# Expert tiles: one of the four result transfers of a tile moved ahead of the second low part on POOL, with waits for ACT's high parts between the transfers

## The chip, the cores and the metric

The kernel runs on one core of one Trainium2 chip. The metric is the device time of one execution in microseconds. The kernel uses all engines of the core: TensorE (PE in the rows, PEld for its weight loads), VectorE (DVE), ScalarE (ACT), GpSimd (POOL) and SyncE (SP), each with its own program and in order; they meet only through semaphores.

## The reference

A network of layers on an input of 32 images of 16 x 16 pixels with 64 channels: a windowed attention, an involution convolution, a linear attention over tokens, a mixture of experts routed per image, another linear attention, and last a mixture of experts routed per token. The change lies in the last one:

```python
flat = x.reshape(-1, C)                      # 8192 tokens, C = 64
probs = softmax(flat @ router_w.T)           # 8 experts
topk_probs, topk_idx = top_k(probs, 2)       # then normalised
h1 = einsum('nc,ehc->neh', flat, w1)         # H = 682
h3 = einsum('nc,ehc->neh', flat, w3)
h = silu(h1) * h3
y = einsum('neh,ech->nec', h, w2)
out = einsum('ne,nec->nc', gates, y)
```

## The kernel before

Each token is sent to the slots of its two experts in a scratch tensor, so that every expert's tokens stand together. The work is then cut into NT = 39 tiles of 512 slots. For a tile t the hidden dimension is cut into NHB = 6 blocks of 114 (index k = 0 to 5), and one block goes through all engines:

- **up product** (TensorE, L2123, four matmuls of 512 columns) into two PSUM banks;
- **silu** (ACT, L1630) of the first bank, then the product with the second (DVE, L1331), the hidden value in float32;
- **high part** (ACT, L1613): the hidden value rounded to float16; the semaphore `high5` counts them, so that `high5` at t * 6 + k + 1 means that the high part of block k of tile t is made;
- **low part**: what the rounding left, hidden value less high part, in float16. For k = 0, 1, 3, 4 DVE makes it (L1341), for k = 2 and 5 POOL (L722, `low5_pool`);
- **down product** (TensorE, L2104, eight matmuls of 128 columns), which waits for the low part. It is issued three blocks behind the up product, so those of k = 3, 4, 5 stand in the next tile, behind its up products of k = 0, 1, 2.

After the last down product of a tile ACT copies one half of the result (L1621) and DVE adds the other (L1347, semaphore `y5`), both in the next tile. At k = 4 TensorE transposes the next tile's input (L2093) and ACT copies it (L1607), from which the next tile's first up product reads.

POOL then sends the 512 finished rows out by four indirect transfers of 128 rows (L710, `results5`), to places that a small copy of ids (L704, `ids5`) made earlier. POOL's program is written out tile by tile in order of t, with no loop. TensorE, ACT and DVE run tiles 2 to 37 in a loop whose turn takes two tiles, an even and an odd one; the tiles at both ends are written out. SP loads the input of a tile (L543) once the input of two tiles before was transposed and its ids copied. After the last transfer has landed, SP loads all results back, and DVE and POOL mix them and write the output.

Of the kernel before, what the change touches and what calls it, by code (L numbers as in the profile page):

```python
# [27 lines left out]
HB, NHB = 114, 6  # L28
# [7 lines left out]
NT = (4 * COLS + E * (SLOTS - 1)) // SLOTS  # L36
# [75 lines left out]
def network(nc, xw_d, xi_d, mats_d, vecs_d, feats_d, cw1_d, wmask_d, taps_d, wexp_d,  # L112
            w1l2_d, w2l2_d, w1l3_d, w3l3_d, w2l3_d, out_d, slots_d, results_d):
    with ExitStack() as ctx:
# [5 lines left out]
        def S(step):  # L120

            name = PLACE.get(step, (step, 0))[0]
            if name not in sems:
                sems[name] = nc.alloc_semaphore(name)
            return sems[name]

        def when(step, n):

            return S(step), PLACE.get(step, (step, 0))[1] + n
# [439 lines left out]
        def _(pool):  # L569
# [130 lines left out]
            def ids5(t):  # L700
                if t >= 4:
                    pool.wait_ge(*when(f"resulted_{t % 2}", 16 * SUB * (t // 2 - 1)))
                pool.wait_ge(*when(f"loaded_xs_{t % 2}", 16 * (t // 2 + 1)))
                nc.gpsimd.tensor_copy(IDS[t % 4], XS[t % 2].bitcast(U32)[:, :, C]).then_inc(S("ids5"), 1)  # L704

            def results5(t, subs):
                pool.wait_ge(*when("y5", t + 1))
                pool.wait_ge(*when("ids5", t + 1))
                for i in subs:
                    pool.indirect_dma_start(  # L710
                        results_d, bass.IndirectOffsetOnAxis(ap=IDS[t % 4][:, i:i + 1], axis=0),
                        Y5[t % 2][:, i, :], None).then_inc(S(f"resulted_{t % 2}"), 16)
# [4 lines left out]
            def low5_pool(t, k):  # L717
                n = t * NHB + k
                pool.wait_ge(*when("high5", n + 1))
                if n >= 3:  # L720
                    pool.wait_ge(*when("down5", n - 2))
                nc.gpsimd.tensor_tensor(LO5[k % 3], H5[k % 3], HI5[k % 3], ALU.subtract).then_inc(S("low5_pool"), 1)  # L722

            for t in range(NT + 1):
                if t < NT:
                    low5_pool(t, 2)
                if t >= 1:
                    results5(t - 1, (0, 1))
                if t < NT:
                    low5_pool(t, 5)  # L730
                if t >= 1:
                    results5(t - 1, (2, 3))
                    if t + 1 < NT:
                        ids5(t + 1)
            for c in (1, 3, 5):
# [1575 lines left out]
```

## Time and profile before

| | us |
|---|---|
| median of three timed runs | 1309.49 (1305.29 to 1313.16) |
| the profiled execution, its own time | 1303.19 |
| its span, first to last instruction | 1301.2 |
| busy in the span: PE, DVE, ACT, POOL | 998.1, 854.9, 689.0, 648.7 |
| stretch of the 39 tiles | about 906 to 1268 |

The rows below are of this one profiled execution, and times in them count from the start of its span. Busy time of an engine doesn't say that it sets the pace; the idle time in brackets behind a row, with what ended it, and the distance between starts say more. "issue" stands for idle time that the profile can't put down to another engine. Times on POOL are rough, so its work is best read by the distance of starts.

### The profile page before, as it was taken

The numbers are of one execution on the slowest core, as the hardware profiler recorded it, in microseconds if no ns is written. First come the engines' busy times: TensorE is split into PE (matmuls) and PEld (weight loads), VectorE is DVE, ScalarE is ACT, GpSimd is POOL, SyncE is SP. The second block draws the span as 40 slices with busy tenths as digits, with TensorE's granted clock in tenths as the row PEclk, the third lists the DMA queues.
The fourth block names the chain that finished last, engine by engine and source line by source line (L and its number), as shares of the span: only waits on it lengthen the run. The fifth ranks groups of instructions, "written<-read, shape, count | busy, mean of one in ns | idle before, by whom it ended". The sixth has DMA issues, their size and how long they took to land.

```text
span 1301.2 us, 23386 instructions
## 1 busy us (share of the span) xinstructions
PE 998.1 (77%) x6350; PEld 631.7 (49%) x6351; DVE 854.9 (66%) x1864; ACT 689.0 (53%) x1311; POOL 648.7 (50%) x722
## 2 busy tenths in 40 slices
PE   5779999948996986667787656521999999999970
PEld 3347777723446752233354334210666666666640
DVE  7977777778857325645746555550777777777757
ACT  2714444405462366555665443211888888878860
POOL 3924545422778202000404456574576767767775
PEclk9979999978998798777898887755999999999995
DMA  5000000010004000000200000011001011010105
GB/s 190 2 1 0 0 0 0 0 60 1 1 28 126 21 1 0 1 0 0 68 5 16 17 20 22 19 36 49 23 26 32 26 31 32 26 32 27 31 22 194
DMA packets 24261, 38.55 MB, mean 30 GB/s; under 512 B 6212, under 2 KB 14168, under 8 KB 23960
## 3 DMA queue, kind: packets, MB, share of 16 engines
q1 hardware_dynamic: 15128, 28.62, 7.0%
q0 software_dynamic: 9088, 9.39, 2.3%
q8 instruction: 21, 0.34, 0.1%
q14 instruction: 24, 0.20, 0.1%
HBM read 24.52 MB, written 13.47 MB: 29 GB/s over the span
## 4 chain that ended last, share of the span: by engine, by line
PE 38%; POOL 17%; DVE 17%; issue 16%; ACT 7%; another core or an unknown queue 2%; SPq 1%; DMA 1%; DVEq 0%; POOLq 0%; ACTq 0%
POOL results L710 10%; POOL stage L722 6%; PE bank L1707 5%; PE bank L1724 4%; PE bank L1716 2%; PE bank L1709 2%; PE bank L1766 2%; PE bank L1931 2%; PE bank L1896 2%; PE bank L1732 1%; DVE T L800 1%; PE bank L1779 1%; PE bank L1915 1%; PE bank L1814 1%
## 5 line engine op out<-in xcount | busy, mean ns | idle before, releaser
L2123 PE MATMUL bank<-stage,big 128*114 128x512 f16 x936 | 244.4, 384 | 21.5 <-issue 20.6
L1331 DVE TENSOR_TENSOR T<-bank,T 114x512 f32<-114x512 f32 x234 | 161.6, 691 | 120.7 <-ACT T L1630 120.2
L687 POOL DMA_INDIRECT slots<-T,index x128 | 124.5, 972 | 118.4 <-DVE index L1242 81.9
L1630 ACT ACTIVATE T<-bank 114x512 f32<-114x512 f32 x234 | 139.8, 597 | 66.1 <-PE bank L2123 43.8
L710 POOL DMA_INDIRECT results<-stage,small x156 | 152.8, 980 | 37.7 <-issue 37.7
L2104 PEld LDWEIGHTS bank<-l2w,stage 114*128 114x128 f16 x1872 | 121.1, 98 | 58.2 <-issue 19.2
L1613 ACT ACTIVATE stage<-T 114x512 f16<-114x512 f32 x234 | 146.1, 625 | 0.3 <-DVE T L1331 0.3
L2104 PE MATMUL bank<-l2w,stage 114*128 x1872 | 143.6, 219 | 1.8 <-POOL stage L722 0.8
L2123 PEld LDWEIGHTS bank<-stage,big 128*114 x936 | 108.6, 132 | 67.9 <-issue 30.8
L722 POOL TENSOR_TENSOR stage<-T,stage 114x512 f16<-114x512 f32 x78 | 90.0, 1153 | 74.4 <-ACT stage L1613 65.2
L1341 DVE TENSOR_TENSOR stage<-T,stage 114x512 f16<-114x512 f32 x156 | 106.3, 681 | 0.0
L1397 ACT ACTIVATE stage<-stage 128x512 f32<-128x512 f32 x64 | 40.3, 630 | 118.8 <-DVE stage L825 118.8
L613 POOL TENSOR_TENSOR stage<-T,vecs 128x128 f32<-128x128 f32 x64 | 26.4, 412 | 105.3 <-PE bank L1709 105.3
L1707 PE MATMUL bank<-stage 128*128 128x512 f32 x128 | 70.0, 628 | 6.7 <-DVE big L810 6.7
L634 POOL TENSOR_TENSOR stage<-stage 128x512 f16<-128x512 f32 x40 | 46.0, 1158 | 51.8 <-ACT stage L1431 50.8
L822 DVE TENSOR_REDUCE small<-bank 128x8 f32<-128x512 f32 x64 | 44.3, 692 | 36.0 <-PE bank L1709 36.0
L617 POOL TENSOR_TENSOR stage<-T,small 128x512 f32<-128x512 f32 x64 | 67.6, 1056 | 0.0
L1724 PE MATMUL bank<-big,stage 128*128 (+1 forms) x512 | 62.8, 268 | 0.0
L1724 PEld LDWEIGHTS bank<-big,stage 128*128 128x128 f32 x512 | 62.2, 192 | 0.1
L1931 PE MATMUL bank<-T,mats 128*128 128x512 f32 x64 | 42.6, 763 | 20.2 <-ACT T L1520 13.6
L672 POOL MEMSET stage<- 128x2080 f32 x1 | 1.8, 1831 | 106.7 <-DVE T L1095 106.7
L1507 ACT ACTIVATE stage<-bank,small 128x256 f32<-128x256 f32 x64 | 30.3, 473 | 43.1 <-PE bank L1915 40.8
(384 smaller groups left out, 2134.4 us busy)
## 6 DMA issues: line engine op xcount, KB each, us to landing
stage<-slots SPq DMA_DIRECT2D x39, 130.0 KB
stage<-in_w1l SPq DMA_DIRECT2D x8, 342.0 KB
stage<-in_w3l SPq DMA_DIRECT2D x8, 342.0 KB
results<-stage,small POOLq DMA_INDIRECT x156
T<-in_xw SPq DMA_DIRECT2D x4, 512.0 KB, 6.9
X<-in_xi SPq DMA_DIRECT2D x1, 2048.0 KB, 14.9
slots<-T,index POOLq DMA_INDIRECT x128
A<-results SPq DMA_DIRECT2D x4, 512.0 KB, 6.6
```

The source lines that it names most:

```text
L687: pool.indirect_dma_start(slots_d, bass.IndirectOffsetOnAxis(ap=index[:, k, n:n + 1], axis=0), rows5[:, n * RW:(n + 1) * RW], None).then_i ...
L710: pool.indirect_dma_start(results_d, bass.IndirectOffsetOnAxis(ap=IDS[t % 4][:, i:i + 1], axis=0), Y5[t % 2][:, i, :], None).then_inc(S(f" ...
L722: nc.gpsimd.tensor_tensor(LO5[k % 3], H5[k % 3], HI5[k % 3], ALU.subtract).then_inc(S("low5_pool"), 1)
L1331: nc.vector.tensor_tensor(H5[q], bank[3 + q][0:HB, :], S5[q], ALU.mult).then_inc(S("hid5"), 1)
L1341: nc.vector.tensor_tensor(LO5[q], H5[q], HI5[q], ALU.subtract).then_inc(S("low5"), 1)
L1613: nc.scalar.activation(HI5[q], H5[q], ACT.Copy).then_inc(S("high5"), 1)
L1630: nc.scalar.activation(S5[q], bank[q][0:HB, :], ACT.Silu).then_inc(S("silu5"), 1)
L1707: nc.tensor.matmul(bank[s][:, :], QB[s], KX[s], start=True, stop=False)
L1724: mm = nc.tensor.matmul(bank[4 + s][:, g * VW:(g + 1) * VW], PT[s][:, g * 128:(g + 1) * 128], VX[:, bass.ds(n * HP + g, 1), :].rearrange(" ...
L1931: nc.tensor.matmul(out, mat("mean"), T2P[c], start=True, stop=True).then_inc(S4(op), 1)
L2104: mm = nc.tensor.matmul(bank[6 + s][:, i * 128:(i + 1) * 128], H[:, i * 128:(i + 1) * 128], downs[:, bass.ds(w, 2 * C)], start=(k == 0 and ...
L2123: mm = nc.tensor.matmul(bank[q + 3 * (v // 2)][0:HB, :], big16[:, bass.ds(e * (4 * HID3) + (v * HID3 + k * HB), HB)], XT[s], start=(v % 2 ...
```

## The change

Before, POOL's program for tile t is: low part of block 2, transfers 0 and 1 of tile t - 1, low part of block 5, transfers 2 and 3, copy of the ids of tile t + 1. After it, transfers 0, 1 and 2 stand between the two low parts, and transfer 3 behind the second. Ahead of transfer 1 POOL waits for `high5` at t * 6 + 4 (block 3 of tile t, counted from 0), ahead of transfer 2 for t * 6 + 5 (block 4). In the last round (t = NT, no tile left) there are no such waits. As `results5` is now called for one transfer at a time, its own two waits (`y5`, `ids5`) are repeated for each.

```diff
                 if t < NT:
                     low5_pool(t, 2)
                 if t >= 1:
-                    results5(t - 1, (0, 1))
+                    for i in range(3):
+                        if i and t < NT:
+                            pool.wait_ge(*when("high5", t * NHB + 3 + i))
+                        results5(t - 1, (i,))
                 if t < NT:
                     low5_pool(t, 5)
                 if t >= 1:
-                    results5(t - 1, (2, 3))
+                    results5(t - 1, (3,))
                     if t + 1 < NT:
                         ids5(t + 1)
```

## Rows read from the trace of the kernel before

**Rows 1.** The page: shares of the chain that ended last, by line.

```profile
POOL results L710 10%; POOL stage L722 6%; PE bank L1707 5%; PE bank L1724 4%; PE bank L1716 2%; PE bank L1709 2%; PE bank L1766 2%; PE bank L1931 2%; PE bank L1896 2%; PE bank L1732 1%; DVE T L800 1%; PE bank L1779 1%; PE bank L1915 1%; PE bank L1814 1%
```

**Rows 2.** Tiles' stretch: busy (PE, PEld, DVE, ACT, POOL), PEclk, DMA; a wait's total, times.

```profile
912.68:1255.99 343.31, 322.73 (x2903) 224.22 (x2902) 257.24 (x421) 280.26 (x535) 240.04 (x261) 1.00 0.10 28
...
POOL stage L722 <- ACT stage L1613: 65.2, 40, 8.1
```

**Rows 3.** POOL's timeline, tile 14: start, duration, line, work, [idle before].

```profile
1039.82 1.15 POOL L722 TENSOR_TENSOR stage<-T,stage 114x512 f16<-114x512 f32 x1 [0.25 <-issue]
1041.13 1.00 POOL L710 DMA_INDIRECT results<-stage,small  x1 [0.16 <-issue]
1042.44 0.96 POOL L710 DMA_INDIRECT results<-stage,small  x1 [0.30 <-issue]
1044.48 1.15 POOL L722 TENSOR_TENSOR stage<-T,stage 114x512 f16<-114x512 f32 x1 [1.08 <-ACT stage L1613]
1045.79 0.99 POOL L710 DMA_INDIRECT results<-stage,small  x1 [0.16 <-issue]
1047.09 0.97 POOL L710 DMA_INDIRECT results<-stage,small  x1 [0.31 <-issue]
...
1048.49 1.16 POOL L722 TENSOR_TENSOR stage<-T,stage 114x512 f16<-114x512 f32 x1 [0.24 <-issue]
```

**Rows 4.** The other engines' timeline in the same stretch.

```profile
1042.03 0.64 ACT L1613 ACTIVATE stage<-T 114x512 f16<-114x512 f32 x1
...
1043.78 0.62 ACT L1613 ACTIVATE stage<-T 114x512 f16<-114x512 f32 x1
...
1044.77 1.03 PE L2123 MATMUL bank<-stage,big 128*114 128x512 f16 x4
...
1045.78 0.62 PE L2104 MATMUL bank<-l2w,stage 114*128 x8
...
1045.92 0.68 DVE L1341 TENSOR_TENSOR stage<-T,stage 114x512 f16<-114x512 f32 x1
...
1046.23 1.03 PE L2123 MATMUL bank<-stage,big 128*114 128x512 f16 x4
...
1047.10 0.61 PE L2104 MATMUL bank<-l2w,stage 114*128 x8
...
1047.79 0.62 ACT L1613 ACTIVATE stage<-T 114x512 f16<-114x512 f32 x1
```

**Rows 5.** POOL's timeline, tile 29, an odd one.

```profile
1174.85 1.15 POOL L722 TENSOR_TENSOR stage<-T,stage 114x512 f16<-114x512 f32 x1 [0.25 <-issue]
...
1178.70 0.96 POOL L710 DMA_INDIRECT results<-stage,small  x1 [1.54 <-issue]
1180.21 1.16 POOL L722 TENSOR_TENSOR stage<-T,stage 114x512 f16<-114x512 f32 x1 [0.54 <-ACT stage L1613]
```

**Rows 6.** Timeline of all engines, the last tile.

```profile
1255.99 1.15 POOL L722 TENSOR_TENSOR stage<-T,stage 114x512 f16<-114x512 f32 x1 [0.24 <-issue]
...
1258.61 0.96 POOL L710 DMA_INDIRECT results<-stage,small  x1 [0.30 <-issue]
...
1259.60 1.17 POOL L722 TENSOR_TENSOR stage<-T,stage 114x512 f16<-114x512 f32 x1
...
1261.97 0.42 DVE L1347 TENSOR_TENSOR stage<-stage,bank 128x256 f32<-128x256 f32 x1 [2.61 <-ACT stage L1621]
...
1263.50 0.97 POOL L710 DMA_INDIRECT results<-stage,small  x1 [0.30 <-issue]
1264.77 0.97 POOL L710 DMA_INDIRECT results<-stage,small  x1 [0.30 <-issue]
1266.04 0.97 POOL L710 DMA_INDIRECT results<-stage,small  x1 [0.30 <-issue]
```

**Rows 7.** The last stage: DVE beside POOL, and alone.

```profile
1287.71 1.53 DVE L1357 TENSOR_TENSOR X<-X,small 128x512 f32<-128x512 f32 x1
...
1296.59 0.68 DVE L1357 TENSOR_TENSOR X<-X,small 128x512 f32<-128x512 f32 x1
```

## The prediction

> **What bounds the kernel now.** I read the page first: no engine is busy all the way, and POOL's transfer line (L710) and low-part line (L722) head the chain that ended last, with 10% and 6% [rows 1]. That invites the thought that POOL sets the pace where the change is. The stretch with the expert tiles must decide, so I took its busy times: in 343.3 us TensorE is busy 322.7 at a granted clock of 1.00 (2.4 GHz), ACT 280, DVE 257, POOL 240 [rows 2]. TensorE is the engine near its limit, POOL has a third of the time free.
>
> Next, POOL's own timeline through one tile [rows 3]. The low part of block 2 starts at 1039.82, two transfers follow, and the queue then stands idle 1.08 us until ACT's high part of block 5 exists (1043.78 + 0.62 = 1044.40; POOL starts 0.08 later, at 1044.48) [rows 3, 4]. The other low part (1048.49) has a gap of 0.24 filed under issue, but it too starts 0.08 after an ACT high part: 1047.79 + 0.62 = 1048.41 [rows 3, 4]. So both low parts are now started by ACT, neither by POOL's queue. The chain's shares name POOL because it was followed back along POOL's own order; they are no room to gain.
>
> Last, what waits for POOL. TensorE's up product of block 2 starts at 1044.77; in tile after tile the down product comes 0.87 after an up product (1046.23 to 1047.10). Here it comes 1.01 after, at 1045.78, which is 0.15 behind the end of POOL's low part (1044.48 + 1.15 = 1045.63) [rows 3, 4]. So the down product of block 5 already waits for POOL, by 0.14 us, and that low part has no slack: whatever it is late by, TensorE is late by. Of the 39 down products behind POOL's other low part none is put down as waiting for it before the last tile.
>
> The distance between the two low parts of a tile is set by ACT and TensorE and has two sizes: about 4.66 us in even tiles (1039.82 to 1044.48 is tile 14; there are eighteen, t = 2 to 36, between 4.63 and 4.70) and 5.36 in odd ones (1174.85 to 1180.21), where the loop of TensorE turns over [rows 3, 5]. From the second low part to the next tile's first it is 4.01 (1044.48 to 1048.49) [rows 3]. The outliers at the ends are t = 0 (no transfers), t = 1 and t = 37 (5.09 and 4.94 in the same view).
>
> **The change, part by part.** It adds two waits per tile and moves one transfer of four from behind the second low part to in front of it. No transfer is added.
>
> *The two waits.* They stand for the high parts with index 3 and 4 of tile t. Index 3 is ready before index 4, and index 4 is ready 2.85 us after the first low part starts (1042.03 + 0.64 = 1042.67) [rows 3, 4]. The second transfer starts 2.62 after it (1042.44), over a microsecond behind index 3, and the third can't start before 3.90 [rows 3]. So neither wait holds: hidden by POOL's own work. If instead they held, by ACT being 1.05 later, they would push the transfer and the low part behind it. The waits as instructions: in the tail, the transfer behind the two repeated waits (1266.04) starts 1.27 after the one before, the one with no wait between (1264.77) 1.27 as well [rows 6]. A satisfied wait is free to within 0.01. For three ahead of one transfer I take 0; the upper end is in a rival.
>
> *The moved transfer.* I add start-to-start distances: low part to first transfer 1.31, to the second 1.31, to the third 1.28 (between 1.30, as 1045.79 to 1047.09, and the tail's 1.27) [rows 3, 6], transfer to low part 0.99. The last is seen once where POOL itself was late: 1258.61 to 1259.60, no idle time put down [rows 6]. The sum is 4.89 us. In even tiles 4.66 are there, so the low part of block 5 comes 0.23 late. In odd tiles 4.89 is under 5.36: nothing. In t = 1 and 37 it just fits. Bounds for the late part: gap from transfer to low part between 0.03 (this row) and 0.30 (a transfer behind a transfer) [rows 3]; that is 0.23 to 0.50 per even tile.
>
> *Does it pass on?* The down product of block 5 moves by the same 0.23, and the up product of block 3 behind it. ACT turns to the silu of block 3 as that product ends (1046.23 + 1.03 = 1047.26) and makes the high part of block 2, which starts the next low part, at 1047.79 [rows 4]; a cover of 0.1 at most can hide there (my estimate: the silu takes 0.6, so it began about when the product ended). I count 0.23 in full: 18 x 0.23 = 4.1 us. Lower bound: ACT's cover hides 0.1 each time, 18 x 0.1 = 1.8 less.
>
> The Trainium skill ("SBUF — State Buffer", section "Who interferes with whom") says that a DVE instruction with two SBUF inputs and a GpSimd instruction that reads SBUF exclude one another. The trace of the last stage agrees: L1357 takes 1.53 us beside POOL and 0.68 alone [rows 7]. By that rule the later low part (ending 1045.86) would come within 0.06 of DVE's L1341 at 1045.92 and could hold it 0.1 or 0.2; the down product that needs it is at 1047.10, 0.50 after its end at 1046.60, so the sum is 4.4 us by the rule and without it.
>
> *What moves earlier.* Behind the second low part only one transfer and the copy of the ids remain: 1.31 + 0.99 + 0.20 of 4.01 us. The copy comes about a microsecond earlier; the load of a later tile that it frees is not waited for. The first low part stays ACT's, so this buys nothing.
>
> *The tail.* In the last tile POOL already was the limit (3.61 us between low parts, 1255.99 to 1259.60) [rows 6]. With three transfers it is 4.89, so 1260.88, 1.28 late. Behind it stand the down product, ACT's copy and DVE's sum, with nothing else to do: the sum, before at 1261.97 for 0.42 us, ends at 1263.67, and the first transfer of the last tile starts at some 1263.8 instead of 1263.50 [rows 6]. The other delays are made up, since POOL had a queue of transfers to work off: +0.3 us.
>
> *A hiccup.* Once in the stretch a transfer came 1.24 late (idle 1.54 against 0.30) and the wait for ACT swallowed it [rows 5]. After the change the same thing between the low parts costs 4.89 + 1.24 - 5.36 = 0.8, or 1.24 in an even tile. I leave it out of the sum and keep it in the range.
>
> Sum: 4.1 + 0.3 = 4.4 us. The profiled execution took 1303.19 us (span 1301.2), so its like would take 1307.6; the median of the three timed runs is 1309.49, 6.3 above it. I predict against the median: 1313.9 us, 0.34% more. A measurement of this kernel tells about 0.5%, 6.5 us, from no change.
>
> **The rivals.**
> - *Later by more.* The gap before the low part is the 0.24 that stands between copy and low part [rows 3], or the three waits cost 0.1 together each time. Then the sum is 5.10, late by 0.44: 18 x 0.44 = 7.9, t = 1 and 37 give 0.2, the tail 0.5: 1318.1 us, slower by 0.66%. For it: that gap is there in every tile. Against it: it ends 0.08 after ACT's high part, and the only gap in which POOL was late is 0.03. It passes 0.5% from 0.34 us per even tile.
> - *Hidden.* The two sizes, 4.66 and 5.36, show that TensorE's loop turn costs 0.7 us every second tile [rows 3, 5]. If that time runs from something earlier than TensorE's last product, the lateness of the tile before vanishes in it. Then 0 to 2 us, 1310.5. Against it: the turn stands in TensorE's own program, behind that product and behind all that was late.
> - *Faster.* If the first low part is in truth held by POOL's queue and the 0.24 before it is its cost, the lighter second half starts it earlier and relieves the down product behind it; and if the 0.14 stall at block 5 went in 37 tiles as well, 5.2 us would be won: 1304.3. It decides only if POOL can start the low part of block 5 before 1044.48, and ACT's high part excludes that: 65.2 us of waiting for L1613 stand against it, in 40 waits [rows 2].
> - *No such order.* That ACT's high parts come late enough to hold the transfers needs index 4 about 1 us later than [rows 4] show before the waits bind at all; bound by 1 us more, the second low part would be late by 1.2 us in an even tile and 0.5 in an odd one, 31 us in all: 1340.
>
> **How the numbers follow.** My forecast (slower by 2.5 to 6 us) 0.58, later by more 0.17, hidden 0.13, faster 0.10, waits that bind 0.02. The range leaves that last one out and takes in the larger gap with a hiccup (1318.1 + 1.2 = 1319.3, and up to 1321 for the scatter of medians) and the hidden case with as much scatter below: 1307 to 1321. The faster rival's 5.2 us are just short of 0.5%, so with scatter and a larger relief I give 0.07 of its 0.10 to faster by over 0.5%; slower by over 0.5% is the 0.19 of the two slow rivals and 0.06 of my own case's upper scatter, 0.25; the rest, 0.68, is within 0.5%.
>
> **What the changed profile would show.** Right: in even tiles three L710 behind the first L722, 1.3 apart, and the second L722 4.9 us after the first with next to no idle time before it and no ACT named; in odd tiles 5.35 as before, with idle time of some 0.4; no transfer waiting for L1613; the down product 0.15 behind the end of that L722; two tiles in 18.27 instead of 18.04 us; behind the second L722 an idle time of over 1 us. Wrong: even distances of 5.1 (first rival), a pair of tiles still 18.04 (hidden) or shorter (faster), or transfers with an ACT wait before them.

## The result, and the profile after

The changed kernel takes 1319.63 us (median of 7 runs, 1315.16 to 1326.39), the kernel before 1310.83 (7 runs on the same chip): ratio of the means 1.0077, 95% interval 1.0047 to 1.0106, so 10 us slower and between 6 and 14 (the medians lie 8.8 apart). The forecast was 1313.9, slower by 4.4 us, and 1319.63 is in its range; but 0.77% is over the 0.5% within which the prediction put its largest chance (0.68), and falls in the 0.25 for slower. The direction and the delay that was worked out are there. The size is about twice the forecast's, and the profile shows a second delay that the prediction doesn't have.

The profiled execution of the changed kernel is the longest of its seven: 1326.39 us, span 1324.4. Its first low part starts at 923.20, against 914.1 in the trace of before: 9.1 of the 23.2 us between the two profiled executions lie ahead of the tiles, where nothing was changed. What counts is the tiles' stretch, from the first low part to the last. It was 345.5 us and is 360.4, and what follows the last low part is 0.8 shorter (40.8 against 41.6), so the traces put 14.1 us on the change, at the upper end of the interval.

First the stretch's busy times, as in [rows 2] but from the first low part to the last, the same of the kernel before (second view), and the waits in it in the changed kernel (in the changed kernel each line behind the edit has a number 3 higher: L1613 is L1616, L2104 is L2107, L2123 is L2126).

```profile
923.20:1283.60 360.40, 328.43 (x2926) 222.57 (x2924) 258.03 (x423) 276.92 (x537) 253.35 (x266) 1.00 0.09 27
```

```profile
914.08:1259.60 345.52, 323.96 (x2919) 224.96 (x2918) 258.60 (x423) 281.87 (x537) 243.16 (x265) 1.00 0.10 28
```

```profile
POOL stage L722 <- ACT stage L1616: 77.4, 60, 7.3
...
ACT T L1633 <- PE bank L2126: 71.8, 110, 1.5
...
PE bank L2107 <- POOL stage L722: 7.4, 19, 0.9
...
PE bank L2107 <- DVE stage L1344: 6.2, 19, 0.7
```

The work is the same and the clock is still 1.00 (2.4 GHz). POOL is busy 10 us longer, most of it in the copy of the ids (0.68 us in place of 0.20 in the even tiles); it has that time free. The stretch is 15 us longer because TensorE waits. Two waits come nineteen times each: for POOL's low part (forecast), in the eighteen even tiles and in tile 29, and for DVE's (not forecast), in sixteen of the even tiles and at the two ends. POOL's timeline of tile 14 answers to [rows 3]:

```profile
1053.35 1.16 POOL L722 TENSOR_TENSOR stage<-T,stage 114x512 f16<-114x512 f32 x1 [1.48 <-ACT stage L1616]
1054.66 1.00 POOL L710 DMA_INDIRECT results<-stage,small  x1 [0.15 <-issue]
1055.97 0.97 POOL L710 DMA_INDIRECT results<-stage,small  x1 [0.30 <-issue]
1057.24 0.97 POOL L710 DMA_INDIRECT results<-stage,small  x1 [0.30 <-issue]
1058.23 1.17 POOL L722 TENSOR_TENSOR stage<-T,stage 114x512 f16<-114x512 f32 x1
1059.56 0.99 POOL L710 DMA_INDIRECT results<-stage,small  x1 [0.16 <-issue]
1060.55 0.65 POOL L704 COPY small<-stage 128x4 uint32<-128x4 uint32 x1
```

The second low part is 4.88 us behind the first (forecast 4.89), right behind the third transfer, with no idle time and no engine named: POOL's own queue starts it now, where ACT did. No transfer waits for ACT. The other engines in the same tile show the second delay:

```profile
1056.90 1.03 PE L2126 MATMUL bank<-stage,big 128*114 128x512 f16 x4
...
1058.21 1.03 PE L2126 MATMUL bank<-stage,big 128*114 128x512 f16 x4
1059.16 0.60 ACT L1633 ACTIVATE T<-bank 114x512 f32<-114x512 f32 x1 [1.22 <-PE bank L2126]
...
1060.48 0.68 DVE L1344 TENSOR_TENSOR stage<-T,stage 114x512 f16<-114x512 f32 x1
...
1061.31 0.62 PE L2107 MATMUL bank<-l2w,stage 114*128 x8 [0.29 <-DVE stage L1344]
```

The up product that starts at 1056.90 ends at 1057.93, but ACT's silu of it starts at 1059.16, 1.2 us later, and ACT was idle for all of that. The silu's product and low part on DVE are late with it, and the down product at 1061.31 waits. That lengthens the distance from the second low part to the next tile's first from 4.01 to 4.44 in the median (4.41 here, 1058.23 to 1062.64). In odd tiles everything is as forecast: below, the third transfer, and then the low part still started by ACT, 0.56 after POOL came free (5.39 from the first, against 5.36):

```profile
1066.54 0.97 POOL L710 DMA_INDIRECT results<-stage,small  x1 [0.30 <-issue]
1068.07 1.15 POOL L722 TENSOR_TENSOR stage<-T,stage 114x512 f16<-114x512 f32 x1 [0.56 <-ACT stage L1616]
```

The last tile, which answers to [rows 6]:

```profile
1283.59 1.17 POOL L722 TENSOR_TENSOR stage<-T,stage 114x512 f16<-114x512 f32 x1
1284.90 0.66 PE L2107 MATMUL bank<-l2w,stage 114*128 x8 [2.09 <-POOL stage L722]
...
1286.01 0.42 DVE L1350 TENSOR_TENSOR stage<-stage,bank 128x256 f32<-128x256 f32 x1 [3.96 <-ACT stage L1624]
1286.70 0.97 POOL L710 DMA_INDIRECT results<-stage,small  x1 [0.79 <-DVE stage L1350]
```

The low part is 4.89 behind the one before (3.61 in [rows 6]), and the first transfer of the last tile starts 3.11 after it (1283.59 to 1286.70) where it was 3.90 (1259.60 to 1263.50): late by 1.28, and 0.8 made up again.

### The profile page after: what moved, and what is told of

It is laid out like the page before. It is cut to its first block, busy times and chain, and to the rows that moved or that the text cites. A ratio compares the mean times of both kernels' runs of the same rounds, so it can differ in the third digit from the quotient of the medians.

```text
span 1324.4 us, 23464 instructions
## 1 busy us (share of the span) xinstructions
PE 1002.2 (76%) x6350; PEld 630.1 (48%) x6351; DVE 855.9 (65%) x1864; ACT 683.4 (52%) x1311; POOL 657.3 (50%) x722
## 4 chain that ended last, share of the span: by engine, by line
issue 38%; PE 30%; DVE 12%; POOL 11%; ACT 5%; DMA 2%; SPq 1%; DVEq 0%; POOLq 0%; ACTq 0%
POOL results L710 6%; PE bank L1710 4%; PE bank L1727 4%; POOL stage L722 3%; PE bank L1719 2%; PE bank L1712 2%; PE bank L1769 2%; PE bank L1899 2%; POOL small L704 1%; PE bank L1735 1%; DVE T L803 1%; PE bank L1782 1%; PE bank L1817 1%; PE bank L1918 1%; DVE small L263 1%
## 5 line engine op out<-in xcount | busy, mean ns | idle before, releaser
L2126 PE MATMUL bank<-stage,big 128*114 128x512 f16 x936 | 243.4, 383 | 18.5 <-issue 15.8
L2107 PEld LDWEIGHTS bank<-l2w,stage 114*128 114x128 f16 x1872 | 118.1, 98 | 79.3 <-issue 53.4
L2107 PE MATMUL bank<-l2w,stage 114*128 x1872 | 143.7, 219 | 15.9 <-POOL stage L722 9.5
L1616 ACT ACTIVATE stage<-T 114x512 f16<-114x512 f32 x234 | 146.6, 626 | 0.2 <-DVE T L1334 0.2
L2126 PEld LDWEIGHTS bank<-stage,big 128*114 x936 | 108.1, 131 | 64.4 <-issue 27.0
L1344 DVE TENSOR_TENSOR stage<-T,stage 114x512 f16<-114x512 f32 x156 | 106.8, 685 | 0.0
L898 DVE TENSOR_TENSOR stage<-bank,big 128x512 f32<-128x512 f32 x72 | 46.9, 688 | 8.8 <-PE bank L1782 6.5
```

Source lines behind the costliest of these rows:

```text
L1344: nc.vector.tensor_tensor(LO5[q], H5[q], HI5[q], ALU.subtract).then_inc(S("low5"), 1)
L1616: nc.scalar.activation(HI5[q], H5[q], ACT.Copy).then_inc(S("high5"), 1)
L2107: mm = nc.tensor.matmul(bank[6 + s][:, i * 128:(i + 1) * 128], H[:, i * 128:(i + 1) * 128], downs[:, bass.ds(w, 2 * C)], start=(k == 0 and ...
L2126: mm = nc.tensor.matmul(bank[q + 3 * (v // 2)][0:HB, :], big16[:, bass.ds(e * (4 * HID3) + (v * HID3 + k * HB), HB)], XT[s], start=(v % 2 ...
```

## The experiments

The ratios compare each with the kernel before on the same chip in the same session. There the kernel before took 1262.17 us (e1 to e4), 1263.92 (e5, e6), 1262.59 (e7b to e9b) and 1303.94 (e10 to e12). Of the kernel before there are two traces only, "before" and e5, so the distances of e1 to e4 and e7b to e9b are read against those of e5. The names in the expectations are: LATE, the late low part of block 5 alone; SIGNALS, TensorE's results being told late while POOL works on transfers directly in a row; WAITS, the added waits.

The table has the distances between POOL's low parts (median; "in" from a tile's first to its second, "out" from there to the next tile's first), the length of a pair of tiles, and the stretch from the first low part to the last.

```
kernel            even in + out  odd in + out   pair   stretch  ratio of times [95%]
before            4.66 + 4.01    5.35 + 4.02    18.05  345.5    
after             4.88 + 4.44    5.39 + 4.01    18.71  360.4    1.0077 [1.0047, 1.0106]
e5 before again   4.53 + 4.01    5.36 + 4.01    17.91  343.2
e6 after again    4.88 + 4.03    5.36 + 4.01    18.28  352.1    1.0049 [1.0031, 1.0068]
e1 order only     4.88 + 4.03    5.36 + 4.01    18.29  352.1    1.0079 [1.0056, 1.0101]
e2 waits only     4.59 + 4.01    5.41 + 4.01    18.02  345.3    1.0021 [1.0001, 1.0041]
e3 filler         4.78 + 4.17    5.53 + 4.02    18.75  360.2    1.0115 [1.0073, 1.0157]
e4 paced pair     4.53 + 4.02    5.36 + 4.02    17.93  344.4    1.0033 [1.0012, 1.0054]
e7b odd only      4.53 + 4.02    5.35 + 4.02    17.92  344.3    1.0015 [0.9997, 1.0033]
e8b all four      6.14 + 4.02    6.13 + 4.03    20.31  391.7    1.0389 [1.0337, 1.0442]
e9b blocks 1, 4   4.24 + 4.16    4.24 + 4.74    17.38  333.5    0.9902 [0.9867, 0.9937]
e10 blocks 0, 3   4.96 + 4.11    5.09 + 4.21    18.35  353.2    1.0041 [1.0017, 1.0065]
e11 blocks 1, 5   6.99 + 2.84    7.03 + 2.84    19.70  376.4    1.0208 [1.0167, 1.0249]
e12 1, 4, three   5.33 + 4.01    5.33 + 4.02    18.72  365.0    1.0113 [1.0056, 1.0169]
```

**e1, the order alone**, and **e2, the waits alone**.

```diff
-                    results5(t - 1, (0, 1))        # e1; (2, 3) becomes (3,)
+                    results5(t - 1, (0, 1, 2))
```

```diff
-                    results5(t - 1, (0, 1))        # e2; (2, 3) one by one
+                    for i in range(2):
+                        if i and t < NT:
+                            pool.wait_ge(*when("high5", t * NHB + 3 + i))
+                        results5(t - 1, (i,))
+                    if t < NT:
+                        pool.wait_ge(*when("high5", t * NHB + 5))
```

> The order of the change without its two waits: low part of block 2, transfers 0, 1, 2, low part of block 5, transfer 3. Three theories stand for the 0.44 us that the changed kernel's even tiles lose behind the second low part (4.45 instead of 4.01), on top of the 0.22 by which that low part is late. SIGNALS: TensorE's semaphore signals are held while POOL works on transfers that follow one another directly, and three in a row hold them past the point where ACT needs one. LATE: the late low part of block 5 alone causes it. WAITS: the two waits do something that costs. SIGNALS and LATE expect this kernel to be like the changed one: even tiles 4.88 + 4.45, odd ones 5.37 + 4.01, about 12 us more than before in the tiles. WAITS expects even tiles of 4.88 + 4.01, some 4 us.

> The kernel before with the two waits added (one ahead of transfer 1, the other ahead of the low part of block 5) and each transfer with waits of its own, no transfer moved. SIGNALS and LATE expect the tiles of before, 4.66 + 4.01 and 5.36 + 4.01, no change in time within 0.2%. WAITS expects a part of the 0.44, over 4 us.

e1 has all of the lateness, 4.88 in every even tile, and it passes on in full: 8.91 an even tile against 8.54 in e5. e2 has 0.06 in even and 0.05 in odd tiles, 2 us on the stretch. The order is the cost; the waits are next to nothing (and e6 below, with order and waits, has e1's stretch to 0.1 us). But in neither is the second delay: the distance out of an even tile is 4.03 in e1 and 4.01 in e2.

**e3, other work in the place of the transfer**: order of before, and a memset of a buffer that is no longer used behind transfer 1.

```diff
                     results5(t - 1, (0, 1))
+                    nc.gpsimd.memset(KVSf[:, 0:1344], 0.0)
```

> The order of before, and behind transfer 1 a memset of unused memory of about 1.27 us, so that the low part of block 5 is as late as in the changed kernel, 4.8 to 4.9 behind the first, with only two transfers in a row ahead of it. LATE expects 4.45 behind it in even tiles, about 12 us in all. SIGNALS expects 4.01 behind it and no late silu of block 1 in odd tiles, 4 us in all.

The stretch is as long as that of after (360.2 against 360.4), but not for the reason sought. The even distance is 4.78, all distances but one are longer, and some transfers take 1.42 to 1.52 us in place of 1.00. The memset is no neutral filler; the run shows that a microsecond more of this other work between the low parts costs too. As no signal is held in it, it says nothing on what holds them.

**e4, a wait that parts the two transfers** of the kernel before.

```diff
-                    results5(t - 1, (0, 1))
+                    results5(t - 1, (0,))
+                    if t < NT:
+                        pool.wait_ge(*when("high5", t * NHB + 5))
+                    results5(t - 1, (1,))
```

> The order of before, with transfer 1 held until ACT's high part of block 4 exists (a wait that binds: transfer 1 some 0.3 us later, no longer directly behind transfer 0). SIGNALS, if the direct succession matters, expects the signal of the down product of block 3, held 0.34 us in the trace of before, to come in time; nothing waits for it, so the time stays within 0.2%. The others expect no change either; it tells what holds the signals.

The wait holds the transfer (idle 0.73 before it), the low part behind it stays ACT's, and all median distances are those of e5. The ratio is nevertheless 1.0033, 4.2 us (1.5 to 6.8), of which the stretch shows 1.2 (344.4 against 343.2). So up to a third of a per cent can come from outside the tiles' stretch, which is the better measure of what an edit does there.

**e5 and e6, both kernels again**, unchanged, with profiles on one chip.

> The kernel before, unchanged, profiled once more: in the trace before the prediction TensorE's signals are held by 0.3 to 0.9 us behind the second of two transfers, and none is held in the traces of the four first experiments. If the holds belong to the order of the program, they are here again, with distances of 4.66, 4.01, 5.36, 4.01 and 18.04 us for two tiles. If they belong to the chip or the execution, they are gone, and two tiles take less, 17.9 to 18.0.

> The changed kernel, unchanged, profiled once more beside it. If its two waits cost 0.44 us in each pair of tiles on any chip, the distances are again 4.88, 4.45, 5.37, 4.01 and the silu of block 1 is late. If that was the chip or the execution, they are those of the order without waits, 4.88, 4.03, 5.36, 4.01, 18.28 for two tiles, and the tiles take some 5 to 8 us more than before.

```profile
1009.80 1.03 PE L2126 MATMUL bank<-stage,big 128*114 128x512 f16 x4
...
1010.19 0.97 POOL L710 DMA_INDIRECT results<-stage,small  x1 [0.30 <-PE bank L2107]
...
1010.95 0.60 ACT L1633 ACTIVATE T<-bank 114x512 f32<-114x512 f32 x1 [0.20 <-PE bank L2126]
1011.12 1.03 PE L2126 MATMUL bank<-stage,big 128*114 128x512 f16 x4
1011.17 1.18 POOL L722 TENSOR_TENSOR stage<-T,stage 114x512 f16<-114x512 f32 x1
...
1012.18 0.60 ACT L1633 ACTIVATE T<-bank 114x512 f32<-114x512 f32 x1
...
1012.49 0.62 PE L2107 MATMUL bank<-l2w,stage 114*128 x8 [0.35 <-POOL stage L722]
1012.52 1.30 POOL L710 DMA_INDIRECT results<-stage,small  x1 [0.17 <-issue]
```

This is the changed kernel with the forecast's delay alone. The low part starts without idle time, TensorE's down product comes 1.37 behind its up product (1011.12 to 1012.49), where 1.01 was before [rows 4], and the silu of the up product ahead of that one (1009.80) starts at 1010.95, 0.12 after the product's end at 1010.83. In the first trace of after this silu is the one that was 1.2 late. The stretch grows by 8.9 us, of which 0.9 comes back in the tail (40.8 us behind the last low part against 41.7).

The same can be counted over the stretch. Of its 234 silus, those that start over 0.8 us after both their up product has ended and ACT has come free:

```
before 0, after 18; e1 to e6, e7b, e8b, e9b: 0 each; e10 17, e11 35, e12 23
```

In before, 35 of them start 0.15 to 0.20 late; in e1 to e9b none is late by 0.15. The semaphore records of the down products agree: 37 of 232 in before, 49 of 233 in after and 31 of 231 in e10 stand over 0.8 us behind the product's end, none in e1 to e9b. (In before, after and e10 to e12 a part of the other signal records of the stretch is missing, on every engine, of the up products 17 of 234 in before and 43 in after; in the other traces none is. So I count silus and not records for the up products.)

So there are executions in which TensorE's signals are held back, and others in which none is, with the same programs. The kernel before takes 1304 to 1311 us where they are held and 1262 to 1264 where they are not; only 2.3 us of that difference is in the tiles' stretch, and of the 37 us between the two profiled executions 35 lie ahead of it (first low part at 914.08 and 879.25).

**e7b, the third transfer ahead in odd tiles alone.**

```diff
+                early = 3 if t % 2 else 2
                 ...
-                    results5(t - 1, (0, 1))
+                    results5(t - 1, range(early))
                 ...
-                    results5(t - 1, (2, 3))
+                    results5(t - 1, range(early, 4))
```

> The order of after (third transfer ahead of the second low part) in odd tiles alone, the order of before in even tiles, no waits added. LATE: in odd tiles the low part has 0.5 us of slack, the third transfer fits in it, nothing is later: distances of 4.53 and 4.01 us in even tiles, 5.36 and 4.01 in odd ones, 17.91 for a pair, ratio 1.000. SIGNALS: three transfers directly in a row in every odd tile still hold up TensorE's signals there; pair 18.1 to 18.4, ratio 1.003 to 1.007.

No median distance moves by more than 0.01. Half of the change is free: the odd tiles have the slack, all but tile 29. There a transfer comes after 1.54 us of idle time, in place of 0.30, as it did in [rows 5], and the low part is late by 0.75 (6.11 in for 5.35). The rest of the cost is in the even tiles.

**e8b, all four transfers ahead.** `results5(t - 1, (0, 1, 2, 3))` between the low parts, only the copy behind.

> All four transfers of a tile ahead of the second low part, no waits added. LATE: the low part starts a fourth transfer (1.27 us) later, so the first distance is 4.88 + 1.27 = 6.15 us in even and in odd tiles, against 4.53 and 5.36 before: 1.62 + 0.79 = 2.41 us a pair, pair 20.3, about 43 us over 18 pairs, ratio about 1.034. SIGNALS: the second distance grows as well, 4.01 to 4.4, and the pair is over 20.7. WAITS (that the waits cost, not the place): there are none here, no change.

6.14 and 6.13 measured, 6.15 expected; pair 20.31, 20.3 expected. The ratio, 1.0389 (1.034 expected), is 49 us (43 to 56), and the stretch is 48.5 longer (391.7 less 343.2): 2.40 x 18 = 43 from the pairs, as expected, and the rest, which the expectation left out, from the single tiles at the ends, the last with 6.13 for 3.62, and from tile 29 (7.37). Four rows of it:

```profile
1059.16 0.96 POOL L710 DMA_INDIRECT results<-stage,small  x1 [0.30 <-issue]
1060.15 1.16 POOL L722 TENSOR_TENSOR stage<-T,stage 114x512 f16<-114x512 f32 x1
1061.25 0.66 POOL L704 COPY small<-stage 128x4 uint32<-128x4 uint32 x1
1064.17 1.16 POOL L722 TENSOR_TENSOR stage<-T,stage 114x512 f16<-114x512 f32 x1 [2.25 <-ACT stage L1612]
```

The fourth transfer, the low part at its end, and after it 2.25 us in which POOL has nothing to do: the time that a transfer costs ahead of the second low part is idle behind it.

**e9b, POOL computes the low parts of blocks 1 and 4** (order of transfers as before).

```diff
-        POOL_LOW = (2, 5)
+        POOL_LOW = (1, 4)
...
-                    low5_pool(t, 2)     # and 5
+                    low5_pool(t, 1)     # and 4
...
             steps3(dve, tile_vector)
+            low5(NT * NHB - 1, (NHB - 1) % 3)
```

> Order of the transfers as before; POOL computes the low parts of blocks 1 and 4 of a tile instead of 2 and 5, VectorE those of 2 and 5. LATE: what binds at block 5 in even tiles is POOL's low part behind two transfers, which begins two blocks after the first; with one block's more time between POOL's low parts and the next tile's, the down products stop waiting for POOL: up to 0.15 us a pair of blocks, at most 5 us of 1264 faster, ratio 0.996 to 1.000. If the place of the low part in the tile isn't what binds, ratio 1.000; if the transfers now fall beside work that they lengthen, up to 1.003.

POOL has blocks 1 and 4, DVE has 0, 2, 3 and 5, so DVE makes one more low part behind the last tile. 1250.51 us, ratio 0.9902: 12 us faster (8 to 17), of which the stretch shows 9.7, more than the 5 at most that LATE allowed. TensorE's timeline shows from where. First the kernel before (e5): an up product and the down product behind it that waits for POOL, the change of tile in an odd tile, and such an up and down product again:

```profile
1044.97 1.03 PE L2123 MATMUL bank<-stage,big 128*114 128x512 f16 x4
1045.97 0.62 PE L2104 MATMUL bank<-l2w,stage 114*128 x8
...
1050.15 0.61 PE L2104 MATMUL bank<-l2w,stage 114*128 x8
1051.67 1.07 PE L2123 MATMUL bank<-stage,big 128*114 128x512 f16 x4 [0.91 <-issue]
...
1054.33 1.03 PE L2123 MATMUL bank<-stage,big 128*114 128x512 f16 x4
1055.35 0.62 PE L2104 MATMUL bank<-l2w,stage 114*128 x8
```

and the same of e9b:

```profile
1052.77 1.03 PE L2124 MATMUL bank<-stage,big 128*114 128x512 f16 x4
1053.70 0.62 PE L2105 MATMUL bank<-l2w,stage 114*128 x8
...
1063.64 0.61 PE L2105 MATMUL bank<-l2w,stage 114*128 x8
1064.85 1.07 PE L2124 MATMUL bank<-stage,big 128*114 128x512 f16 x4 [0.59 <-issue]
```

The distance from the up product to the down product that waits for POOL goes from 1.00 and 1.02 to 0.93 (unhindered 0.87), twice a pair: 0.17 us. The change of tile in odd tiles goes from 1.52 (1050.15 to 1051.67) to 1.21 (1063.64 to 1064.85), the one in even tiles from 0.69 to 0.63: 0.37. Together 0.54 a pair; 17.91 less 17.38 is 0.53. Two thirds of the gain in the stretch are thus from the changes of tile, which I had taken for a fixed cost; why they are shorter is not shown.

**e10, e11 and e12** were to split that gain: POOL has blocks 0 and 3 (e10), blocks 1 and 5 with three transfers between and one behind (e11), blocks 1 and 4 with three transfers between (e12). e10 is e9b's edit with other numbers; e11 and e12 join such an edit with e1's.

> Order of the transfers as before; POOL computes the low parts of blocks 0 and 3, VectorE the other four. With blocks 1 and 4 a pair of tiles took 17.38 us against 17.91: 0.18 of it from the down products behind POOL's second low part (a wait of 0.06 left in place of 0.15), 0.37 from the two places where TensorE goes over to the next tile (1.52 to 1.21, 0.69 to 0.63). TURN: the turn runs from the end of the low part that the last down product before it waits for, that of block 2; VectorE makes it here too, so the turns stay at 1.21 and 0.63 and the pair is 17.3 to 17.5, ratio 0.988 to 0.992. PLACE: it is the place of POOL's low parts in the tile that counts, one block earlier once more takes off up to 0.5 us a pair: ratio 0.980 to 0.986; or, if it puts a low part against the turn, adds some.

> POOL computes the low parts of blocks 1 and 5, with three transfers between them and one behind; no waits added. TURN: VectorE makes the low part of block 2, so the turn in odd tiles falls from 1.52 to 1.21 though block 5 stays POOL's; four blocks lie between the low parts, 5.5 us, and three transfers with a low part need 4.88: they fit. Pair 17.4 to 17.6, ratio 0.990 to 0.995. LATE: as for the distances, but with the turn unchanged: pair 17.6 to 17.9, ratio 0.995 to 1.000.

> POOL computes the low parts of blocks 1 and 4, and the third transfer stands ahead of the second low part, as in the change; no waits added. LATE: the low parts are 4.24 us apart in even and in odd tiles when nothing is late, and three transfers take 4.88: 0.64 late in every tile, no tile has slack. Pair 17.38 + 1.28 = 18.66, ratio to before 1.008 to 1.011: the same move costs 1.28 us a pair here where it cost 0.37 with blocks 2 and 5. If instead the lateness is taken up by the turn, 18.0 to 18.3, ratio 0.999 to 1.004.

In these runs TensorE's signals were held, and they answer another question than they were made for. e10: neither 0.98 nor 0.99, but 1.0041. A row of POOL shows what is against its order:

```profile
1055.39 1.01 POOL L710 DMA_INDIRECT results<-stage,small  x1 [1.50 <-DVE stage L1347]
```

With the low part of block 0 first, the transfers come up before DVE has made the sum that they send (36 such waits, 55 us), and the second low part behind them is late: 4.96 in. e11 expected 1.000 at most and came to 1.0208: four blocks lie between its low parts, and they are 7.0 us apart, not 5.5. Its rows:

```profile
1055.26 1.07 PE L2123 MATMUL bank<-stage,big 128*114 128x512 f16 x4
...
1055.84 0.97 POOL L710 DMA_INDIRECT results<-stage,small  x1 [0.30 <-issue]
...
1057.72 0.60 ACT L1630 ACTIVATE T<-bank 114x512 f32<-114x512 f32 x1 [1.28 <-PE bank L2123]
1057.93 1.03 PE L2123 MATMUL bank<-stage,big 128*114 128x512 f16 x4
...
1058.92 1.15 POOL L722 TENSOR_TENSOR stage<-T,stage 114x512 f16<-114x512 f32 x1 [2.11 <-ACT stage L1613]
```

POOL waits 2.11 us for ACT, ACT 1.28 for TensorE, though the up product of 1055.26 ended at 1056.33. Three transfers in a row stand before it (1053.25, 1054.56, 1055.84), and the silu starts 1.9 us after the third. TensorE in turn waits for the late low part (36 times, 31.5 us), and the next low part, at 1061.76, starts without idle time behind POOL's copy, so both signals and POOL's queue are in the 1.0208. e12 has the late silu too:

```profile
1048.72 1.03 PE L2124 MATMUL bank<-stage,big 128*114 128x512 f16 x4
...
1050.64 0.97 POOL L710 DMA_INDIRECT results<-stage,small  x1 [0.30 <-issue]
...
1051.58 0.60 ACT L1631 ACTIVATE T<-bank 114x512 f32<-114x512 f32 x1 [1.56 <-PE bank L2124]
```

The silu is 1.83 behind the end of its up product (1049.75 to 1051.58). The ratio, 1.0113, and the pair, 18.72, are near the forecast of LATE (1.008 to 1.011, 18.66), but the distances aren't: 5.33 in, not 4.88. The number was right for another reason, and I don't count it for LATE.

## Why the prediction was right, and what it missed

*What bounds.* Right. Ahead of the change ACT started both low parts, and TensorE waited for the one of block 5. e9b confirms it from the other side: with POOL's low parts elsewhere the kernel gets faster.

*The two waits.* Right: no transfer waits for ACT in after, and e1, without waits, has the distances of e6, with them. In e2 they are worth 0.06 us a tile at most, inside the 0.1 that the first rival kept for them.

*The moved transfer.* 4.89 was the sum of start distances, 4.88 is measured, in all three profiles with this order (after, e1, e6), and the sum carried on by one more transfer is right to 0.02 in e8b. The lateness was mis-sized by the other side of the difference: 0.22 on the first chip (forecast 0.23), but 0.35 in e6, since before is at 4.53 where no signal is held. In the first trace signals some 0.15 late had already taken 0.13 of the loss. No row of before shows that the low parts of an even tile can be 4.53 apart.

*Does it pass on?* Right, in full, and only in even tiles (e6: 8.91 against 8.54; e7b: none in odd ones). Of e6's 8.9 us on the stretch, 0.37 x 18 = 6.7 are this term, 1.3 the last tile and 0.85 tile 29.

*The missed term.* The step that failed is the sum's "4.1 + 0.3", in which every distance behind the second low part stays at 4.01; the prediction says why it gets no shorter and gives no reason that it can't grow. In after there are another 0.43 us an even tile, 0.43 x 18 = 7.7, which don't come from POOL's low part being late but from TensorE's signals, held until the third transfer was well under way or over (the silu starts 1.9 us after that transfer's start in after and e11, 0.9 in e12), so that the silu, DVE's low part and the next down product are late. 18 x (0.22 + 0.43) + 1.28 for the last tile less 0.8 in the tail is 12.2 of the 14.1 us between the traces; 0.8 more is the hiccup below.

The measured times don't show this term apart: e1, with the order alone and no signal held, is at 1.0079, the result at 1.0077, and e6 at 1.0049, with an interval that overlaps both of theirs. With none held the traces still give 8.0 us (8.9 less 0.9), nearly twice the forecast, from the 0.35 in place of 0.23 and tile 29. That the time is in the range is in part luck. "Later by more" gave 1318.1, near the time, but for a gap of 0.24 that isn't there: the low part follows the transfer with no idle time.

*What held the signals* is open. Shown: it isn't the order or the waits alone (e1, e2, e6: 0 held) and isn't needed for the change to cost (e6: 1.0049). It comes in whole executions, and in those it goes with POOL's transfers: all 93 late silus of after, e10, e11 and e12 belong to up products that end after POOL has started the second or third transfer of a row and before its next other instruction, and so do all 37 late down products of before; of all up products of after it is 67 of 234. There are more of the late silus with three transfers in a row (18, 35, 23) than with two (0, 17). The records number the chips: e1 to e4 ran on the one numbered 10 with none held, e10 to e12 on the one numbered 10 with many, e5 and e6 on 3, e7b to e9b on 7. Either the number is shared by chips of several machines or a chip changes; no run here tells.

*The tail* is right: 1.28 late as forecast, 0.8 to 0.9 of it made up behind, which leaves 0.4 to 0.5 (0.3 forecast). *The hiccup* is there (in tile 29 of after, 1193.89 to 1200.09, a transfer comes after 1.62 us idle and the distance is 6.20 for 5.39) and costs 0.8, as said. But it is no accident of one execution, and belonged in the sum: it stands in tile 29 in before, after, e1, e2, e3, e5, e6, e7b, e8b, e9b and e12. What makes it is not shown. *What moves earlier* bought nothing, as said.

*The rule on DVE and POOL* was set aside as changing nothing, and for TensorE's wait that holds. The cost moved to what stands behind the low part: the copy of the ids takes 0.65 us in after, started 0.07 behind DVE's L1344, and 0.20 in an odd tile without it; the transfer behind the late low part takes 1.30 in e6 instead of 1.00. In e6 all 19 transfers that take over 1.15 start while DVE's low part runs. POOL has the slack for both. The Trainium skill ("SBUF — State Buffer", section "Who interferes with whom") has the exclusion for an instruction with two SBUF inputs, and by the copy the trace agrees.

## What to carry to other kernels

An engine's queue that is idle in the mean isn't free at every place: ask for each instruction what starts it and how long it could have been late, tile by tile. Here the odd tiles, all but one, took the transfer for nothing and the even ones passed on all of it, and the second half of POOL's round stood idle for as long as the first was overfull. The better lever was the one that the same reading offers from the other side: give POOL blocks whose down products come when its queue has had time. That was worth 1% (e9b, where no signal was held); with held signals it was not measured.

A time difference between two traces is to be read in the stretch that was changed. Two executions of the kernel before that are 37 us apart in all (1303.19 and 1266.15) had that stretch within 2.3 us.

## What the runs showed of the hardware

- TensorE's signals to other engines can come 0.8 to 2.0 us after the product's end, most of them for products that end while POOL issues indirect transfers directly in a row, in some executions of a program and in others of the same program not at all (down products' signals over 0.8 us late: 37 in before and 49 in after, 0 in e5 and 0 in e6).
- The change from one tile to the next in TensorE's program isn't a fixed cost: 1.52 and 1.21 us for the same instructions. The next up product in even tiles starts 0.43 after ACT's copy of the turned tile in both kernels (1059.78 to 1060.21 and 1055.44 to 1055.87), so there it is ACT that ends it. For the odd tiles the split was tried in e10 and e11 and is open, as their signals were held.
- Four indirect transfers in a row start 1.32, 1.26 and 1.26 us apart (e8b), and the work behind the last starts 0.99 after it.
